# A GRU recurrence's state update: a fourth slot in the state scan rounds the new state to a grid; ScalarE makes the high f16 part and VectorE the low part

## The reference

```python
h0 = hidden_states.mean(axis=1) @ ctx_w.T + ctx_b
xw = hidden_states @ gru_w_ih.T
def step(h, xw_t):
    hw = h @ gru_w_hh.T                    # (8, 1024) @ (1024, 3072)
    xr, xz, xn = jnp.split(xw_t, 3, axis=-1)
    hr, hz, hnn = jnp.split(hw, 3, axis=-1)
    r = jax.nn.sigmoid(xr + hr)
    z = jax.nn.sigmoid(xz + hz)
    n = jnp.tanh(xn + r * hnn)
    h_new = (1.0 - z) * n + z * h
    return (h_new, h_new)
_, hs = jax.lax.scan(step, h0, jnp.swapaxes(xw, 0, 1))
```

## Time and profile before

| what | value |
|---|---|
| median of 3 runs | 4206.03 us (4203.85 to 4216.75) |
| the profiled execution's own time | 4177.58 us |
| its span, first to last instruction | 4175.9 us |
| PE busy | 3861.0 us (92%), 76838 matmuls |
| PE weight loads | 2489.3 us (60%) |
| DVE busy | 3101.5 us (74%) |
| ACT busy | 1518.1 us (36%) |
| POOL busy | 162.8 us (4%) |
| mean TensorE clock | 0.977 of full speed |

### The profile page before, as it was taken

One profiled execution on the slowest core, in us unless ns is written; L12 is line 12 of the kernel. 1 busy time (PEld: TensorE's weight loads), 2 busy tenths in 40 slices (PEclk: granted clock), 3 DMA queues, 4 the chain that ended last, 5 costly groups with the idle time before them and its releaser, 6 DMA issues. The chain is left out here.

```text
span 4175.9 us, 179312 instructions
## 1 busy us (share of the span) xinstructions
PE 3861.0 (92%) x76838; PEld 2489.3 (60%) x76838; DVE 3101.5 (74%) x14963; ACT 1518.1 (36%) x5125; POOL 162.8 (4%) x399
## 2 busy tenths in 40 slices
PE   3999599999999999999999999999999999998999
PEld 3777456666665666566566566566566566655665
DVE  2788677777777777777777777777777777777555
ACT  1122333333344433333333333333333433343222
POOL 1211000000000000000000000000000000000000
PEclk5999799999999999999999999999999999999999
DMA  2011300000000000000000000000000000000000
GB/s 68 18 38 51 141 11 3 3 3 3 3 3 3 3 3 3 3 3 3 3 3 3 3 3 3 3 3 3 3 3 3 3 3 3 3 22 16 10 10 13
DMA packets 46764, 51.49 MB, mean 12 GB/s; under 512 B 11956, under 2 KB 39860, under 8 KB 46004
## 3 DMA queue, kind: packets, MB, share of 16 engines
q1 hardware_dynamic: 46004, 40.48, 3.1%
HBM read 36.28 MB, written 4.19 MB: 10 GB/s over the span
## 5 line engine op out<-in xcount | busy, mean ns | idle before, releaser
L904 PE MATMUL psum<-room,h_parts 128*32 128x384 f16 x65536 | 2770.2, 327 | 137.0 <-DVE h_parts L1033 137.0
L904 PEld LDWEIGHTS psum<-room,h_parts 128*32 128x32 f16 x65536 | 1663.9, 97 | 1160.1 <-DVE h_parts L1033 359.5
L989 DVE STREAM_TRANSPOSE turned<-psum 128x128 f32<-128x128 f32 x1024 | 324.6, 317 | 522.0 <-PE psum L904 522.0
L1093 ACT ACTIVATE r_by<-gates 128x32 f32<-128x32 f32 x1024 | 253.1, 247 | 1151.7 <-DVE gates L968 1151.7
L747 DVE CUSTOM_DVE_ANT_0 products<-routes 128x128 f32<-128x128 f32 x1855 | 478.8, 271 | 4.4 <-ACT routes L740 3.3
L1016 DVE TENSOR_TENSOR_SCAN state<-w_by,state 128x96 f32<-128x96 f32 x1024 | 366.7, 358 | 130.2 <-ACT state L1099 0.8
L1102 ACT ACTIVATE state<-state 128x32 f32<-128x32 f32 x1024 | 255.4, 249 | 435.2 <-DVE state L1016 435.2
L1007 DVE TENSOR_TENSOR_SCAN pre_n<-r_by,n_terms 128x96 f32<-128x96 f32 x1024 | 366.7, 358 | 23.9 <-ACT r_by L1093 2.6
L968 DVE TENSOR_TENSOR gates<-turned 128x32 f32<-128x32 f32 x2048 | 375.3, 183 | 0.0
L999 DVE STREAM_TRANSPOSE n_terms<-psum 128x128 f32<-128x128 f32 x1024 | 333.7, 326 | 0.0
L1099 ACT ACTIVATE state<-pre_n 128x32 f32<-128x32 f32 x1024 | 259.3, 253 | 137.9 <-DVE pre_n L1007 3.4
(11 more groups left out here) (163 smaller groups left out, 2635.0 us busy)
## 6 DMA issues: line engine op xcount, KB each, us to landing
xs_room<-in_L_ffn_gru_w_hh_dram SPq DMA_DIRECT2D x16, 1536.0 KB, 6.6
room<-in_L_attn_x_dram SPq DMA_DIRECT2D x8, 256.0 KB, 5.4
x_scratch<-room SPq DMA_DIRECT2D x8, 256.0 KB, 2.3
room<-x_scratch SPq DMA_DIRECT2D x32, 64.0 KB, 2.2
out_dram<-room SPq DMA_DIRECT2D x32, 64.0 KB, 2.0
xs_room<-in_L_ffn_gru_w_ih_dram SPq DMA_DIRECT2D x3, 512.0 KB, 5.5
xs_room<-in_L_ffn_gate_w_dram SPq DMA_DIRECT2D x7, 128.0 KB, 2.4
xs_room<-in_L_ffn_up_w_dram SPq DMA_DIRECT2D x7, 128.0 KB, 2.5
```

The lines of the kernel that those rows point to most:

```text
L904: last = nc.tensor.matmul(psum[32 * j:32 * j + 32, bank_of(k, half), 0:3 * P], h_parts[:, q, c, :], w_hh_s[:, s, half, 4 * c + j, :, :].re ...
L989: nc.vector.transpose(turned[:, half, 0, :], gate_bank(k, half, 0)).then_inc(r_turned[half], 1)
```

## The change

The state scan gets a fourth slot, with the factor 1 in `w_by` and the constant `TO_GRID` = 1.5 * 2^25 in the added term, so that its fourth output is h_new + TO_GRID. An f32 of that size holds only multiples of 4, so this output minus TO_GRID is h_new rounded to a multiple of 4, which f16 holds. ScalarE subtracts TO_GRID and writes the high part (semaphore `hi_ready`); VectorE computes (slot 3 - TO_GRID) - slot 2, the low part with its sign reversed (semaphore `h_ready`). Neither reads the other's result. The reversed sign is undone where the contributions are summed (subtractions in place of additions) and in the identity for the history; the order of high and low places is swapped too, and the middle factor in `r_by` becomes -1.

The scan's output `state` and its added term `h_terms` are now two buffers, each single. The terms -h and h for the next step are written by ScalarE over both halves at once, after the history copy (semaphore `carried`), in place of the negation in each half. PE waits for both `h_ready` and `hi_ready` of a half.

```diff
-        state = sb("state", [P, 2, CH * B, 3])
+        state = sb("state", [P, CH * B, 4])
+        h_terms = sb("h_terms", [P, CH * B, 4])
-        w_by = sb("w_by", [P, 2, HB, 3])
+        w_by = sb("w_by", [P, 2, HB, 4])
-        ident_16 = sb("ident_16", [P, P], F16)
+        ident_16 = sb("ident_16", [P, 2, P], F16)
...
-                nc.gpsimd.tensor_copy(ident_16[:, :], ident[:, :])
+                nc.gpsimd.tensor_copy(ident_16[:, 1, :], ident[:, :])
+                nc.gpsimd.tensor_scalar(ident_16[:, 0, :], ident[:, :], -1.0, None, ALU.mult)
...
                     pe.wait_ge(h_ready[0], t1)
+                    pe.wait_ge(hi_ready[0], t1)
                     state_share(k, 0, range(0, HALF))
                     pe.wait_ge(bank_free[1], t1)
                     state_share(k, 1, range(0, EARLY))
                     pe.wait_ge(h_ready[1], t1)
+                    pe.wait_ge(hi_ready[1], t1)
...
                     by_part = turned[:, half, g, :].rearrange("p (k f) -> p k f", f=4)
-                    return nc.vector.tensor_tensor(gates[:, half, g, :], by_part[:, :, 2 * q], by_part[:, :, 2 * q + 1], ALU.add)
+                    return nc.vector.tensor_tensor(gates[:, half, g, :], by_part[:, :, 2 * q + 1], by_part[:, :, 2 * q], ALU.subtract)
...
                     dve.wait_ge(n_done[half], t1)
                     dve.wait_ge(w_done[half], t1)
-                    dve.wait_ge(negated[half], t1)
-                    nc.vector.tensor_tensor_scan(row(state[:, 1 - q, here, :]), row(w_by[:, half, :, :]), row(state[:, q, here, :]),
+                    dve.wait_ge(carried, t1)
+                    nc.vector.tensor_tensor_scan(row(state[:, here, :]), row(w_by[:, half, :, :]), row(h_terms[:, here, :]),
                                                  0.0, ALU.mult, ALU.add).then_inc(new_state[half], 1)
...
-                def to_high(t1, k, half):
+                def to_low(t1, k, half):
                     q = k % 2
                     dve.wait_ge(new_state[half], t1)
-                    nc.vector.tensor_copy(part(parts_of(q, half), 2 * (1 - q)), full_of(q, half)).then_inc(hi_done[half], 1)
-
-                def to_low(t1, k, half):
-                    q = k % 2
-                    dve.wait_ge(hi_done[half], t1)
-                    nc.vector.tensor_tensor(part(parts_of(q, half), 2 * (1 - q) + 1), full_of(q, half),
-                                            part(parts_of(q, half), 2 * (1 - q)), ALU.subtract).then_inc(h_ready[half], 1)
+                    nc.vector.scalar_tensor_tensor(part(parts_of(q, half), 2 * (1 - q)), slot_of(half, 3), TO_GRID, slot_of(half, 2),
+                                                   ALU.subtract, ALU.subtract).then_inc(h_ready[half], 1)
...
                     to_state(t1, k, 0)
                     turn_r(t1, k, 1)
-                    to_high(t1, k, 0)
+                    to_low(t1, k, 0)
                     turn_z(k, 1)
-                    to_low(t1, k, 0)
                     to_candidate(t1, k, 1)
                     dot(e, 2 if q == 0 else NSHIFT + 1)
                     to_state(t1, k, 1)
-                    to_high(t1, k, 1)
                     to_low(t1, k, 1)
...
                         act.wait_ge(new_state[half], t1)
-                        nc.scalar.mul(state[:, 1 - q, here, 1], state[:, 1 - q, here, 2], -1.0).then_inc(negated[half], 1)
+                        nc.scalar.activation(part(h_parts[:, 1 - q, half * HALF:(half + 1) * HALF, :], 2 * (1 - q) + 1),
+                                             by_chunk(state[:, here, 3]), ACT.Copy, bias=-TO_GRID).then_inc(hi_ready[half], 1)

                     act.wait_ge(h_ready[1], t1 + 1)
+                    act.wait_ge(hi_ready[0], t1 + 1)
+                    act.wait_ge(hi_ready[1], t1 + 1)
...
                     nc.scalar.copy(history[:, :, :, k, :], now).then_inc(kept, 1)
+                    nc.scalar.mul(h_terms[:, :, 1], state[:, :, 2], -1.0)
+                    nc.scalar.copy(h_terms[:, :, 2], state[:, :, 2]).then_inc(carried, 1)
```

More of the change, by code:

```diff
@@ L702, in sandwich @@
         r_done, w_done, pre_done, n_done = two("r_done"), two("w_done"), two("pre_done"), two("n_done")
-        new_state, negated, hi_done = two("new_state"), two("negated"), two("hi_done")
+        new_state, hi_ready = two("new_state"), two("hi_ready")
+        carried = sem("carried")
         kept = sem("kept")
@@ L790, in _ @@
                 dve.wait_ge(cleared, 2)
-                first_h = state[:, 0, :, 2]
+                first_h = h_terms[:, :, 2]
                 full = by_chunk(first_h)
@@ L813, in _ @@
                 nc.vector.tensor_scalar(neg_unscale[:, :], unscale[:, :], -1.0, None, ALU.mult)
-                nc.vector.tensor_scalar(state[:, 0, :, 1], first_h, -1.0, None, ALU.mult)
-                nc.vector.tensor_copy(part(h_parts[:, 0, :, :], 0), full)
+                nc.vector.tensor_scalar(neg_h_scale[:, :], h_scale_f, -1.0, None, ALU.mult)
+                nc.vector.tensor_scalar(h_terms[:, :, 1], first_h, -1.0, None, ALU.mult)
+                nc.vector.tensor_copy(part(h_parts[:, 0, :, :], 1), full)
                 dve.drain()
-                nc.vector.tensor_tensor(part(h_parts[:, 0, :, :], 1), full, part(h_parts[:, 0, :, :], 0), ALU.subtract)
+                nc.vector.tensor_tensor(part(h_parts[:, 0, :, :], 0), part(h_parts[:, 0, :, :], 1), full, ALU.subtract)
                 for i in range(4):
                     dve.wait_ge(x_first, i + 1)
-                    nc.vector.scalar_tensor_tensor(token_part(i, 1), tokens(i), h_scale_f[:, 0:1], token_part(i, 0),
-                                                   ALU.mult, ALU.subtract)
+                    nc.vector.scalar_tensor_tensor(token_part(i, 0), tokens(i), neg_h_scale[:, 0:1], token_part(i, 1),
+                                                   ALU.mult, ALU.add)
                 dve.drain()
@@ L828, in _ @@
                     dve.sem_inc(bank_free[half], 1)
-                    dve.sem_inc(negated[half], 1)
+                    dve.sem_inc(hi_ready[half], 1)
                 dve.sem_inc(kept, 2)
+                dve.sem_inc(carried, 1)
                 dve.sem_inc(wrap_read, 1)
@@ L967, in summed, with row @@
                     by_part = turned[:, half, g, :].rearrange("p (k f) -> p k f", f=4)
-                    return nc.vector.tensor_tensor(gates[:, half, g, :], by_part[:, :, 2 * q], by_part[:, :, 2 * q + 1], ALU.add)
-                def row(triples):
-                    return triples.rearrange("p k three -> p (k three)")
+                    return nc.vector.tensor_tensor(gates[:, half, g, :], by_part[:, :, 2 * q + 1], by_part[:, :, 2 * q], ALU.subtract)
+                def row(groups):
+                    return groups.rearrange("p k slots -> p (k slots)")
                 def turn_xn(pairs):
@@ L1098, in step @@
                         act.wait_ge(pre_done[half], t1)
-                        nc.scalar.activation(state[:, q, here, 0], pre_n[:, half, :, 2], ACT.Tanh,
+                        nc.scalar.activation(h_terms[:, here, 0], pre_n[:, half, :, 2], ACT.Tanh,
                                              scale=by_unscale).then_inc(n_done[half], 1)
                         act.wait_ge(new_state[half], t1)
-                        nc.scalar.mul(state[:, 1 - q, here, 1], state[:, 1 - q, here, 2], -1.0).then_inc(negated[half], 1)
+                        nc.scalar.activation(part(h_parts[:, 1 - q, half * HALF:(half + 1) * HALF, :], 2 * (1 - q) + 1),
+                                             by_chunk(state[:, here, 3]), ACT.Copy, bias=-TO_GRID).then_inc(hi_ready[half], 1)
                     act.wait_ge(h_ready[1], t1 + 1)
+                    act.wait_ge(hi_ready[0], t1 + 1)
+                    act.wait_ge(hi_ready[1], t1 + 1)
                     if k == 0:
```

22 lines of the change are left out of this document (12 added, 10 removed).

## The result

The change makes the kernel faster by 0.75%: the ratio to the kernel before is 0.9925, with a 95% interval of 0.9906 to 0.9945; medians 4164.7 us and, in the same measurement, 4191.3 us before. The forecast was faster, by 96 us; measured were 27 by the medians and 31 by the ratio, about a third. The time lies in the range of 4078 to 4178 us only by its upper end, which stands for a gain of 28 us over 4206, and the kernel before was itself 15 us quicker in this measurement than those 4206. That the time is in the range is therefore nothing to the forecast's credit.

The account below looks back on a forecast made before the run. Both halves' chains were taken as critical in the recurrence, half B deciding after the change. Its 0.21 us a step, taken as 0.20 over 480 steps, gave 96 us off the median 4206: 4110 us, range 4078 to 4178.

Parts of the forecast that it names:

- What bounds the kernel: Recurrence step: both halves' chains are critical at once; after the change half B's parts, at 1509.43 against A's 1509.36, decide.
- The tile's first step: One step in 16, where PE also turns the history: PE bounds it, so the change leaves it unchanged.
- The state scan: VectorE's scan, from 96 to 128 elements: 0.07 us longer than 0.36, bounds 0 to 0.12.
- The order on VectorE: Cast gone from VectorE's queue: half B's scan 0.05 us earlier, both makers of its parts starting together at 1509.14.
- The low part: VectorE's operation with two subtractions and a constant: 0 more taken, bounds 0 to 0.06 us.
- The high part on ScalarE: In place of the negation in each half: 0.25 us, bounds 0.23 to 0.35, the upper for an operand read per partition.
- PE's wait for two semaphores: Before each half's products, two semaphores instead of one: priced at 0, upper end 0.05 us.
- The sum: PE's load of half B 0.21 us earlier a step; 0.20 taken over 480 steps, 96 us.
- Rival 1: Smaller gain through a scan paying 0.12 or a high part of 0.35: 0.08 us a step, 38 us, 4168; chance 0.19.
- The set-up: A few short instructions more, once: about 1 us, under POOL's and DVE's waits there.
- The carry: ScalarE's negation and carry of h behind the history copy: free by 2.3 us, cost 0; 6 us if not covered.
- The signs: If right: idle before L904 from 128 to about 30 to 60 us, B's load 0.2 us sooner, period 6.03 us.

Follow-up runs that it names:

- e1: Changed kernel with one semaphore per half, counted up by both makers, so PE waits once: recurrence 3128.8 us, ratio to the kernel before 0.9834.
- e6: The e1 version with VectorE making both parts, high first, and ScalarE none: recurrence 3204.9 us.
- e4: Kernel before with a second PE wait per half, for the cast's semaphore, written ahead of the low part's wait: recurrence 3251.2 us.
- e8: Kernel before with a second PE wait for the cast's semaphore, written behind the low part's wait: recurrence 3207.5 us against 3207.0.
- e7: The e1 version with one more small ScalarE instruction before the carry in steps 4 to 10 of each tile, in seven forms: recurrence 3129.1 us.
- e2: Changed kernel with PE's two waits of each half in the other order, hi_ready first: recurrence 3153.4 us.

## Why the prediction was wrong

- **What bounds the kernel**: right. Half B's chain decides; with A's first product at 2.53 us after the first turn and 1.95 us of products, A would be ready at 4.48, and B's come at 4.62. The tile's first step did not move (6.75 us before and after), as forecast. Its third step, counted as a full one, gained only 0.02 us (e1: 0.11).
- **The state scan**: right, 0.425 us against a forecast 0.36 + 0.07.
- **The order on VectorE**: right. B's makers were forecast at 4.19 us after the first turn (1509.14 against the first turn of the earlier trace rows's step, in the line below) and start at 4.20 by the rows. The low part costs what it did, 212 ns.

```profile
1504.95 0.32 DVE L989 STREAM_TRANSPOSE turned<-psum 128x128 f32<-128x128 f32 x1 [0.76 <-PE psum L904]
```

- **The high part on ScalarE**: the term was 0.25 and is 0.28, within its bounds (0.23 to 0.35), for another reason than the operand they allowed for: wider strides of source and target, not the constant. The Trainium skill ("ScalarE: Activation LUTs", section "Rules for kernel authors") sends additions to VectorE; e6 measured that here, and it costs 0.16 us a step (6.225 against 6.065): 0.05 of it in half B, where two short instructions in turn on VectorE end later than a longer one on ScalarE beside one on VectorE, and 0.11 through half A, where VectorE's later work stands behind one instruction more.
- **PE's wait for two semaphores**: here the forecast failed. "I price it at 0; 0.05 (one release latency) is the upper end." Measured: 0.09 to the first product, in both halves of e4 and in half B of the changed kernel against e1 (0.08 in its half A). The row that I took the 0 from was VectorE's state scan with three waits, which starts 0.03 us behind the tanh. But there the wait that ends last is written *first*, and e8 shows that such an order is free on PE; in the changed kernel it is written last. The trace before shows that VectorE's queue splits its waits alike: the waits for w and the negation, written last, are one separate instruction (1024, once per half of a step), and by its semaphores the scan itself carries only the wait for the tanh. The w of a step ends about 0.4 us ahead of its tanh, so that row could only show the cheap order.

```profile
L1015 DVEq EVENT_SEMAPHORE  x1024: 49/144/212, 539.7 to 3746.8; - x171
```

- **The sum**: half B's first product was to come 0.21 us earlier. Less 0.03 for ScalarE and 0.09 for the separate wait that leaves 0.09; measured are 0.08 (4.697 to 4.618 us after the first turn), and 0.083 in the period. The last 0.01 is the release itself, 0.05 where the sum had 0.04. Over 480 steps that is 40 us; measured 38, as the third step of a tile hardly gains. Rival 1 had this size (0.08 a step, 38 us) with a second wait in it, at 0.19; its main causes, a scan of 0.48 us and a pointer operand, did not occur.
- **The set-up**: here the forecast failed too, by a smaller sum. the "about 1 us, under POOL's and DVE's waits there" was taken from no row; measured are 8 us, by GpSimd's two idle gaps around the second identity. The chain of the set-up goes through GpSimd, so they fall on the time whole.
- **The carry**: free, as forecast; no row shows VectorE waiting for it, and e7 adds 0.2 us to it at no cost.
- With the wait mended (e1) the gain is 78 us by the recurrence, of the 96 forecast. The rest is the 0.03 of ScalarE (14 us) and the third step of each tile (3 us).
- **The signs**: one that was to show the forecast right came out as said, PE's idle time before the products falling to 30 to 60 us (44.8), though the gain did not come: most of that idle time only moved behind half A's products, where no row shows it. The two that count the gain failed: PE's first load of B 0.10 us sooner in place of 0.2 (4.59 against 4.69), period 6.15 in place of 6.03.

## What to carry to other kernels

Count waits per instruction, not only what is waited for: on PE an extra wait in front of the instruction on the critical chain cost 0.09 us here, a 51 ns instruction and its dispatch, unless its semaphore was up well ahead (0.3 us was enough, 0.05 was not). Let parallel producers count up one semaphore, where none of them can run a step ahead of the others, or write the wait that ends last first. And before a gain is expected from splitting a serial pair over two engines, price what makes them independent: here the longer scan took back all of it until the second engine was used. Read the set-up in the trace as well: one more instruction off the loop cost 8 us, a fifth of what the loop won.

## What was not expected of the hardware

- Two waits on PE: the one written last appears as a separate 51 ns instruction on its queue; 0.143 to 0.146 us from the last maker to the first product if that one ends last, 0.103 if the other does 0.05 us later (e2), 0.051 to 0.056 with a single wait.
- ScalarE over 32 elements: 227 ns dense to dense, 258 from a 16-byte stride, 271 into an f16 target with a stride of 8 bytes, 273 with both; a conversion to dense f16 together with an added constant written as a number cost 1 ns (e7).
- A PE stall of 0.14 us inside a run of short products shows nowhere in the idle column; it has to be read from the distance between a maker's end and the next weight load.
- GpSimd's second identity in the set-up, 0.57 us long, came with 6.8 to 7.7 us of idle time before it and 5.8 to 6.2 behind it in all eight traces that have it, with no releaser shown.
